# Attention and feed-forward block: keys and queries turned together, their operands filled by transfers, bias and shift rows turned on VectorE

## The reference, cut to what matters

```python
q = rmsnorm((x @ Wq) per head, q_rms_w);  k = rmsnorm((x @ Wk) per head, k_rms_w);  v = (x @ Wv) per head
gate = softplus(einsum('bthd,hd->bht', k, u_n) / 8)
bias = -dist * softplus(omega) * slope * gate        # dist = max(i - j, 0), gate at key j
attn = softmax(q k^T / 8 + bias, causal)
x = layernorm(x + (attn v) @ Wproj)
x = layernorm(x + ffn(x))
```

## Time and profile before

| | |
|---|---|
| time, median of 3 runs | 3689.66 us (3685.36 to 3691.62) |
| the profiled execution, its own time | 3688.23 us |
| its span, first to last instruction | 3686.4 us |
| TensorE busy | 3318.4 us (90%) |
| VectorE, ScalarE, GpSimd busy | 1923.1 (52%), 1868.7 (51%), 1518.6 us (41%) |
| mean granted TensorE clock | 0.954 of 2.4 GHz |
| attention, 92 to 2500 us | TensorE busy 2156 of 2408 us |

### The profile page before, as it was taken

How to read it: one execution, slowest core, us unless ns; L and a number is a source line. 1 busy time by engine, 2 the same in 40 slices (tenths; PEclk the granted TensorE clock), 3 DMA queues, 4 the chain that set the end, 5 groups by cost and what they waited for, 6 DMA issues and landing times. The chain is left out here.

```text
span 3686.4 us, 46240 instructions
## 1 busy us (share of the span) xinstructions
PE 3318.4 (90%) x16112; PEld 2537.8 (69%) x16112; DVE 1923.1 (52%) x4064; ACT 1868.7 (51%) x3185; POOL 1518.6 (41%) x1318
## 2 busy tenths in 40 slices
PE   4989989889899898898988989877999999899999
PEld 3756757667576675665766757656888787688887
DVE  6576566665766757656666576623222222233232
ACT  1666666666666666665666666653222222232222
POOL 4556556555565565555655556541111111000000
PEclk7999999999999999999999999988999999899999
DMA  1111111111112011011111110124222222221120
GB/s 53 32 40 24 37 31 30 38 25 31 40 37 48 24 37 39 22 36 31 30 38 25 31 40 23 37 72 134 83 83 83 83 89 86 70 97 59 45 69 18
DMA packets 138680, 179.90 MB, mean 49 GB/s; under 512 B 37712, under 2 KB 70096, under 8 KB 138448
## 3 DMA queue, kind: packets, MB, share of 16 engines
q1 hardware_dynamic: 138448, 176.94, 17.3%
HBM read 83.81 MB, written 42.47 MB: 34 GB/s over the span
## 5 line engine op out<-in xcount | busy, mean ns | idle before, releaser
L340 POOL TENSOR_TENSOR e_lo<-e_all,e_hi 128x512 fp32r<-128x512 f32 (+1 forms) x832 | 1041.7, 1257 | 948.4 <-ACT e_all L566 792.3
L566 ACT ACTIVATE e_all<-ps_s,bias 128x512 f32<-128x512 f32 (+3 forms) x1280 | 781.4, 619 | 183.5 <-PE ps_s L865 120.5
L559 ACT ACTIVATE e_hi<-ps_s,bias 128x512 fp32r<-128x512 f32 (+1 forms) x832 | 557.7, 670 | 326.9 <-PE ps_s L863 212.8
L747 DVE TENSOR_REDUCE maxes<-ps_m 128x1 f32<-128x512 f32 x768 | 525.2, 686 | 364.0 <-PE ps_m L838 359.6
L838 PE MATMUL ps_m<-k_ext,q_max 128*128 128x512 f32 (+3 forms) x1280 | 486.2, 393 | 61.5 <-DVE maxes L747 38.7
L862 PE MATMUL ps_s<-q_twice,k_split 128*128 128x512 f32 (+3 forms) x1280 | 493.3, 385 | 0.0
L863 PE MATMUL ps_s<-q_ext,k_ext 128*128 128x512 f32 (+3 forms) x1280 | 480.4, 375 | 0.0
L896 PE MATMUL ps_v<-e_lo,v_main 128*66 128x512 f32 (+1 forms) x832 | 441.2, 530 | 15.6 <-POOL e_lo L340 15.6
L838 PEld LDWEIGHTS ps_m<-k_ext,q_max 128*128 128x128 f32 x1280 | 249.5, 195 | 213.3 <-DVE maxes L747 75.2
L744 DVE CUSTOM_DVE_ANT_0 ps_m<-ps_m,mask_row 128x128 f32<-128x128 f32 (+3 forms) x512 | 252.4, 493 | 247.5 <-PE ps_m L838 243.5
L885 PE MATMUL ps_v<-e_hi,v_main 128*66 128x512 f32 (+1 forms) x832 | 331.5, 398 | 0.0
(11 more groups left out here) (211 smaller groups left out, 6517.4 us busy)
## 6 DMA issues: line engine op xcount, KB each, us to landing
q_twice<-q_max SPq DMA_DIRECT2D x256, 128.0 KB, 2.3
yt<-y_out SPq DMA_DIRECT2D x128, 130.0 KB
k_split<-k_ext SPq DMA_DIRECT2D x128, 128.0 KB, 2.2
y_in<-yt SPq DMA_DIRECT2D x128, 128.0 KB, 3.1
r_in<-recip_sums SPq DMA_DIRECT2D x128, 128.0 KB, 3.2
hidden<-gelu SPq DMA_DIRECT2D x64, 256.0 KB, 2.0
a_in<-hidden SPq DMA_DIRECT2D x8, 2048.0 KB, 10.5
x_tok<-in_L_attn_x_dram SPq DMA_DIRECT2D x8, 512.0 KB, 4.8
```

Source lines behind the costliest of these rows:

```text
L340: on.tensor_tensor(e_lo[:, i % LO_RING, off:QB], e_all[:, u_ % E_RING, off:QB], e_hi[:, i % HI_RING, off:QB].bitcast(F32), ALU.subtract).t ...
L559: nc.scalar.activation(e_hi[:, i % HI_RING, off:QB], ps_s[u_ % 2][:, off:QB], ACT.Exp, bias=by).then_inc(hi_done, 1)
L566: nc.scalar.activation(e_all[:, u_ % E_RING, off:QB], ps_s[u_ % 2][:, off:QB], ACT.Exp, bias=by).then_inc(ex_done, 1)
L747: nc.vector.tensor_reduce(maxes[:, qt, kc:kc + 1], ps_m[m % 2][:, 0:width], AX.X, ALU.max).then_inc(mx_free, 1)
```

## The change

- Keys and queries of a head lie beside each other in `raw` (128 columns), and one turn of four transposes brings both; a head has 4 turns, due 0.066 apart, in place of 8 due 0.033 apart.
- ScalarE writes the hi parts of both into `kq_hi`, VectorE the lo parts into `kq_lo` (two buffers each). Transfers on SyncE's queue bring them to `k_ext`, `q_max`, `k_split` (hi) and `k_split`, `q_ext` (lo): five in place of one. The first `max` of a block now waits for `hi_dup`, the landing of the three hi transfers, where it waited for ScalarE.
- The 4 bias columns of each key part leave `raw` (2 columns of logits remain, so 386 in place of 392). VectorE transposes them in blocks of 32 x 32 once a pair, four transfers store them in DRAM (`rows_dram`), and one for each head brings them into `k_ext`. The first `max` of a head also waits for that one.
- The shift row is transposed on VectorE in blocks of 32 x 32; four transfers bring it in place of one. TensorE has no `shift` step any more.
- `project`, `turn` and the transposes of the second batch (`x`) alternate between the banks `ps_p` and `ps_t`, and each waits for the step two before.

```diff
-NTURN = 2 * NQB
+NTURN = NQB
+SQ = 32
...
-            turns = [first + 0.005 + 0.033 * i for i in range(NTURN)]
+            turns = [first + 0.005 + 0.066 * i for i in range(NTURN)]
             for i, when in enumerate(turns):
                 at(when, "turn", n, i)
-            start, end = (turns[1] + 0.03, t0 + 0.28) if s == 0 else (t0 + 0.29, t0 + 1.29)
+            start, end = (turns[0] + 0.07, t0 + 0.28) if s == 0 else (t0 + 0.29, t0 + 1.29)
             for v, (qt, kc) in enumerate(MAXES):
                 qb = qt // TQ
-                when = max(start + (end - start) * v / (NM - 1), turns[2 * qb + 1] + 0.03)
+                when = max(start + (end - start) * v / (NM - 1), turns[qb] + 0.07)
                 at(when, "max", n, v)
                 if v + 1 == maxes_to(qb):
                     at(when + 0.001, "most", n, qb)
-                    at(when + 0.03, "shift", n, qb)
+                    at(when + 0.002, "shift", n, qb)
...
+        works = [s for s in steps if s[0] in ("project", "turn") or s[0] == "x" and s[1] == 1]
+        work_no = {step: i for i, step in enumerate(works)}
+        GATE = 2 + 8 + 14 + 2 + 2 + 1
...
-        def project_bank(p, t):
-
-            return ps_v[1] if p == 0 and t % 2 else ps_p
+        def work_bank(step):
+            return (ps_p, ps_t)[work_no[step] % 2]
+
+        def work_free(eng, step):
+
+            if work_no[step] < 2:
+                return
+            kind, a, b = works[work_no[step] - 2]
+            if kind == "x":
+                eng.wait_ge(xt_done, NXT * a + b + 1)
+            if kind == "project":
+                eng.wait_ge(pj_free, TT * a + b + 1)
+            if kind == "turn":
+                eng.wait_ge(tr_free, NTURN * a + b + 1)
 
...
                     sp.dma_start(w_in[:, :, CV:WCOLS], wv[:, cols].rearrange("(k p) c -> p k c", p=P)).then_inc(w_load, 16)
                     for s in range(2):
                         head = p % (H // 2) * 2 + s
-                        sp.dma_start(w_in[:, :, k_cols(s):k_cols(s) + D],
-                                     wk[:, head * D:(head + 1) * D].rearrange("(k p) c -> p k c", p=P)).then_inc(w_load, 16)
+                        for c, w in ((k_cols(s), wk), (q_cols(s), wq)):
+                            sp.dma_start(w_in[:, :, c:c + D], w[:, head * D:(head + 1) * D].rearrange("(k p) c -> p k c", p=P)).then_inc(w_load, 16)
+                if step[0] == "gate b" and step[2] == GATE_PARTS - 1:
+                    p = step[1]
+                    sp.wait_ge(gate, GATE * (p + 1))
+                    for i in range(2):
+                        if p >= 1:
+                            sp.wait_ge(rows_in[i], 16 * p)
+                    for a in range(P // SQ):
+                        sp.dma_start(rows_dram.rearrange("c r a j -> a r c j")[a],
+                                     bias_out[a * SQ:(a + 1) * SQ, :].rearrange("r (c j) -> r c j", j=SQ)).then_inc(rows_out, 16)
                 if step[0] == "turn":
-                    n, i = step[1:]
-                    s, qc = n % 2, i // 2
-                    if i % 2 == 0:
-                        cols = slice(qc * QB, (qc + 1) * QB)
-                        sp.wait_ge(qk_hi, NTURN * n + i + 1)
-                        sp.dma_start(k_split[s][0:D, cols].bitcast(F32), k_ext[s][0:D, cols].bitcast(F32)).then_inc(k_dup[s][qc], 16)
+                    n, qb = step[1:]
+                    s, i = n % 2, NTURN * n + qb
+                    cols = slice(qb * QB, (qb + 1) * QB)
+                    sp.wait_ge(qk_hi, i + 1)
+                    sp.dma_start(k_ext[s][0:D, cols].bitcast(F32), kq_hi[i % 2][0:D, :].bitcast(F32)).then_inc(hi_dup[i % 2], 16)
+                    sp.dma_start(q_max[s][0:D, cols].bitcast(F32), kq_hi[i % 2][D:P, :].bitcast(F32)).then_inc(hi_dup[i % 2], 16)
+                    if qb == 0:
+                        sp.wait_ge(rows_out, 16 * (P // SQ) * (n // 2 + 1))
+                        sp.dma_start(k_ext[s][R_BIAS:R_BIAS + NBIAS, :].bitcast(F32), rows_dram[:, s * TT:(s + 1) * TT, :, :].rearrange("c r a j -> c (r a j)")).then_inc(rows_in[s], 16)
+                    sp.dma_start(k_split[s][0:D, cols].bitcast(F32), kq_hi[i % 2][0:D, :].bitcast(F32)).then_inc(hi_dup[i % 2], 16)
+                    sp.wait_ge(tr_free, i + 1)
+                    sp.dma_start(k_split[s][D:P, cols].bitcast(F32), kq_lo[i % 2][0:D, :].bitcast(F32)).then_inc(lo_dup[i % 2], 16)
+                    sp.dma_start(q_ext[s][0:D, cols].bitcast(F32), kq_lo[i % 2][D:P, :].bitcast(F32)).then_inc(lo_dup[i % 2], 16)
                 if step[0] == "twice":
                     n, qb = step[1:]
                     s, grp = n % 2, n * NQB + qb
                     cols = slice(qb * QB, (qb + 1) * QB)
-                    sp.wait_ge(qk_hi, NTURN * n + 2 * qb + 2)
+                    turned(sp, n, qb)
...
+                    sp.wait_ge(shifted, grp + 1)
+                    for a in range(P // SQ):
+                        row = q_ext[n % 2][R_SHIFT:R_SHIFT + 1, qb * QB:(qb + 1) * QB].bitcast(F32).rearrange("o (t p) -> o t p", t=TQ)
+                        sp.dma_start(row[:, :, a * SQ:(a + 1) * SQ], shift_rows[grp % 2][a * SQ:a * SQ + TQ, :]).then_inc(row_in[grp % 2], 16)
...
+                    n, qb = step[1:]
+                    i = NTURN * n + qb
+                    act.wait_ge(tr_full, i + 1)
+                    if i >= 2:
+                        act.wait_ge(hi_dup[i % 2], 48 * (i // 2))
+                        act.wait_ge(tr_free, i - 1)
+                    nc.scalar.activation(kq_hi[i % 2][:], work_bank(step)[:], ACT.Copy, scale=qk_w[:, 0:1]).then_inc(qk_hi, 1)
                 if step[0] == "scores":
                     n, v = step[1:]
                     u_ = NU * n + v
@@ -607,7 +647,7 @@
...
+                        glink(nc.vector.tensor_copy(bias_in[:, :, 0, :, :], c_jc[:]))
+                        glink(nc.vector.tensor_tensor(bias_in[:, :, 1, :, :], c_jc[:], bias_in[:, :, 0, :, :].bitcast(F32), ALU.subtract))
+                        if p >= 1:
+                            dve.wait_ge(rows_out, 16 * (P // SQ) * p)
+                        glink(nc.vector.transpose(bias_out[:], bias_in[:].rearrange("p x h s t -> p (x h s t)").bitcast(F32)))
                         assert gated[0] == GATE * (p + 1), gated[0]
                 if step[0] == "bias":
...
+                    n, qb = step[1:]
+                    i = NTURN * n + qb
+                    dve.wait_ge(qk_hi, i + 1)
+                    if i >= 2:
+                        dve.wait_ge(lo_dup[i % 2], 32 * (i // 2))
+                    nc.vector.scalar_tensor_tensor(kq_lo[i % 2][:], work_bank(step)[:], qk_w[:, 0:1], kq_hi[i % 2][:].bitcast(F32),
+                                                   ALU.mult, ALU.subtract).then_inc(tr_free, 1)
...
                     n, qb = step[1:]
                     dve.wait_ge(mx_free, NM * n + maxes_to(qb))
-                    if n >= 1:
-                        dve.wait_ge(tr_full, turn_no["shift", n - 1, qb] + 1)
-                    nc.vector.tensor_reduce(neg_max[:, qb * TQ:(qb + 1) * TQ], maxes[:, qb * TQ:(qb + 1) * TQ, 0:qb + 1],
+                    grp = n * NQB + qb
+                    if grp >= 2:
+                        dve.wait_ge(shifted, grp - 1)
+                    nc.vector.tensor_reduce(neg_max[grp % 2][:, 0:TQ], maxes[:, qb * TQ:(qb + 1) * TQ, 0:qb + 1],
                                             AX.X, ALU.max, negate=True).then_inc(nm_done, 1)
...
-                    dve.wait_ge(tr_full, turn_no[step] + 1)
+                    dve.wait_ge(nm_done, grp + 1)
                     if grp >= 2:
-                        dve.wait_ge(row_in[grp % 2], 16 * (grp // 2))
-                    nc.vector.tensor_copy(shift_rows[:, grp % 2, :], ps_t[0:TQ, 0:P]).then_inc(tr_free, 1)
+                        dve.wait_ge(row_in[grp % 2], 16 * (P // SQ) * (grp // 2))
+                    nc.vector.transpose(shift_rows[grp % 2][:], neg_max[grp % 2][:].bitcast(F32)).then_inc(shifted, 1)
...
                 if step[0] == "turn":
-                    n, i = step[1:]
-                    s = n % 2
...
+                    n, qb = step[1:]
+                    col = k_cols(n % 2)
...
-                    if turn_no[step]:
-                        pe.wait_ge(tr_free, turn_no[step])
-                    col, width = ((k_cols(s), KCOLS), (s * D, KCOLS))[i % 2]
+                    work_free(pe, step)
                     for t in range(TQ):
-                        last = nc.tensor.transpose(ps_t[0:width, t * P:(t + 1) * P], raw[:, (i // 2) * TQ + t, col:col + width], ident[:])
+                        last = nc.tensor.transpose(work_bank(step)[:, t * P:(t + 1) * P], raw[:, qb * TQ + t, col:col + 2 * D], ident[:])
                     last.then_inc(tr_full, 1)
...
-                        pe.wait_ge(qk_hi, NTURN * n + 2 * (qt // TQ) + 2)
+                        turned(pe, n, qt // TQ)
+                        if qt == 0:
```

(53 more changed lines are left out.)

96 lines of the change are left out of this document (37 added, 59 removed).

## The result

The changed kernel takes 3590.43 us (median of 4 runs, 3587.56 to 3598.06) where the kernel before, beside it, takes 3689.14: the ratio is 0.9737, with a 95% interval of 0.9719 to 0.9754. The forecast was 3595, the range 3560 to 3665. The profiled execution has a span of 3588.1 us.

What follows compares the result with a forecast made beforehand. TensorE's work and waits were taken to bound attention, except ahead of the gate, where VectorE paces. 77.5 + 61.0 - 6 - 32 (landings) - 3 (gate chain) - 3 (first pair) = 94.5 us saved: 3595 us, range 3560 to 3665.

Steps and rivals of the forecast that it cites:

- Two stages: Attention pair: savings count in the 120 us TensorE paces, not in the 30 us ahead of the gate, where VectorE is full.
- one of the signs: Ahead of the gate: the prediction is wrong if the 30 us of VectorE's stage change length.
- Work, 77.5 us: TensorE in attention: fewer turns save 58.9 us, shift transposes gone 14.6 us, narrower projection 4 us.
- Waits, 61.0 us less 6: TensorE's waits for ps_t and negative maxima that count go, 61.0 us; 6 us return as waits for ScalarE or VectorE.
- rival 4: Saved work reappears as waits for VectorE, whose stage ahead of the gate begins earlier: 3673 us, chance 0.07.
- Landings, 2.0 us a pair: Even head's first max of blocks 0 and 1 waits for transfers: cost 32 us, ends 18 and 86.
- the walk: SyncE's queue from the gate, issue by issue: stalls of 0 to 0.4 and 1.1 to 1.5 us at blocks 0 and 1.
- Gate chain, +0.2 us a pair: VectorE's last instructions before the gate: casts and subtractions become one each plus a block transpose, costing 3 us.
- DMA pieces of 128 bytes: Bias stores and shift rows: short pieces expected to land no later than 2 KB ones, against the skill's 512-byte rule.
- rival 5: Short pieces make store and load of the bias rows slow, 3.4 us more before the first max: 3649, chance 0.03.
- The sum: Whole kernel: the terms together save 94.5 us, giving a forecast of 3595 us.
- Of the rivals, 2: Landings, with stalls near 5.4 us a pair, take the gain back in large part: 3662 us, chance 0.20.

Runs made afterwards that it cites:

- e4: Changed kernel with six max matmuls of each odd head, just ahead of the gate, made four times instead of once: 3599.9 us, ratio 0.9773.
- e5: Changed kernel with six max matmuls of each odd head, in the middle of the even head's scores, made four times: 3650.2 us, ratio 0.9906.
- e10: Changed kernel with the shift row transposed on TensorE again, copied by VectorE and moved by one transfer: 3604.4 us, ratio 0.9772.
- e3: Changed kernel with every turn's four transposes made twice into the same place: 3632.9 us, ratio 0.9847.
- e1: Kernel before the change, with only project, turn, shift and the second batch's transposes alternating between two banks: 3629.1 us, ratio 0.9832.
- e6: Changed kernel with the first max of a block due 0.12 of a head behind its turn, not 0.07: 3563.0 us, ratio 0.9668.
- e7: Changed kernel with the first max of a block due 0.03 of a head behind its turn, not 0.07: 3642.1 us, ratio 0.9883.
- e11: Changed kernel with the even head's turns due 0.38 of a head before its start, not 0.46: 3578.3 us, ratio 0.9705.

## Why the prediction was right, and where its terms were not

**Two stages.** Right, and shown by e4 and e5: the same kind of matmuls cost next to nothing in a pair ahead of the gate and 3.4 us elsewhere. e10 shows the same of waits. The stage kept its length, which was one of the signs: from the end of the first wait for maxima to the gate it is 26.0 us before the change and 25.3 after it (mean of 15 pairs).

**Work, 77.5 us.** e3 gives a turn 0.42 us of busy time (53.5 us in all; 42 us of device time) where I had 0.46 (58.9); e10 gives the shifts 13 us with their waits where I had 14.6 + 3.7. The 4 us of the narrower projection were not tested. TensorE's busy time fell by 102 us, more than 77.5. A part may be time around a wait that counts as busy: in e1 it fell by 15 us with no instruction less. The rest stays open.

**Waits, 61.0 us less 6.** The waits went and were worth 58 us alone (e1). But the 6 us that I took back was the term mis-sized most: waits for maxima rose by 39.5 us, by 47 outside the 30 us ahead of a gate, and the wait at the gate by 38 where 28 was forecast, so all of TensorE's waits in attention together did not fall. 33 us of them show behind the odd head's turns, 24 to 55 us behind the gate, where these two stand in the pair shown and others like them in the rest:

```profile
1399.35 0.50 PE L879 MATMUL ps_m<-k_ext,q_max 128*128 128x512 f32 x1 [1.30 <-DVE maxes L786]
...
1404.26 0.50 PE L879 MATMUL ps_m<-k_ext,q_max 128*128 128x512 f32 x1 [0.84 <-DVE maxes L786]
```

With the pause for `ps_t` gone, TensorE reaches VectorE's next maximum sooner; no run here takes VectorE's work away there, so this reading is argued from the trace and not shown. It is what rival 4 said in part, that saved work comes back as waits for VectorE, though it had them ahead of the gate.

**Landings, 2.0 us a pair.** Right in place, less than I took in size: 0.27 and 1.54 us in the pair shown, which is above the mean, and 22.3 us in all, 4.2 us of it in the first pair. The other 15 pairs have 1.2 us each, near the low end of the walk's 1.1 to 1.9. The first `max` of block 1 waits in all of them, that of block 0 in only 5. e6 and e7 show that the landings are on the path; the later due time gives 27 us back, 1.7 a pair, and the clock is a part of that. Odd heads and block 2 show none, and outside the first pair none is over 2.2 us.

**Gate chain, +0.2 us a pair.** Near for an undisturbed chain, wrong in sign on the mean. From the end of the last norm to the last gate instruction's end it is 1.29 us in all 16 pairs after the change. Before it, it is 1.19 us in 10 pairs and 2.8 to 2.9 us in 6, in the mean 1.8, so the change gains 0.5 us a pair, some 8 us. The block transposes take 0.31 us (128 x 128) and 0.21 us (128 x 32). In each of the 6 pairs two instructions of the end took 0.9 to 1.25 us beside GpSimd. After the change, then one of the 6 before it, then one of the 10:

```profile
1355.43 2.67 POOL L366 TENSOR_TENSOR e_lo<-e_all,e_hi 128x512 fp32r<-128x512 f32 x2 [0.87 <-ACT e_all L606]
...
1360.76 0.19 DVE L749 TENSOR_TENSOR c_jc<-g,omega_eff 128x32 f32<-128x32 f32 x1
1360.98 0.19 DVE L751 TENSOR_TENSOR c_jc<-c_jc,key_no 128x32 f32<-128x32 f32 x1
...
1361.70 0.31 DVE L757 STREAM_TRANSPOSE bias_out<-bias_in 128x128 f32<-128x128 f32 x1
```

```profile
1262.71 2.66 POOL L340 TENSOR_TENSOR e_lo<-e_all,e_hi 128x512 fp32r<-128x512 f32 x2 [0.40 <-ACT e_all L566]
...
1263.33 1.17 DVE L708 TENSOR_TENSOR raw<-g,omega_eff 128x32 f32<-128x32 f32 x1
1264.53 0.92 DVE L710 TENSOR_TENSOR raw<-raw,key_no 128x32 f32<-128x32 f32 x1
```

```profile
964.07 0.22 DVE L708 TENSOR_TENSOR raw<-g,omega_eff 128x32 f32<-128x32 f32 x1
964.32 0.22 DVE L710 TENSOR_TENSOR raw<-raw,key_no 128x32 f32<-128x32 f32 x1
```

TensorE now stands 5.9 us at the gate, and GpSimd has run out of work at 1358.1 and holds nothing up. The two go together in every pair: before the change TensorE waits 1.7 to 2.7 us at the gate in the 6 pairs with the long end and 4.2 us or more in the others, and in e10 the end is 2.96 us in the 5 pairs with a wait of 1.9 to 2.2 us, 1.96 us in the 2 pairs with 3.1, and 1.3 us in those with 3.3 or more. A TensorE that comes early and waits long leaves the end of the chain undisturbed. This is the reverse of what e11 ran into.

**DMA pieces of 128 bytes.** The bias stores land after 1.5 us, sooner than any transfer shown before, and no `max` waits for the load of the rows, so rival 5 is out. The rule of the Trainium skill (DMA: Bandwidth & Descriptors, Specifications) on pieces below 512 bytes doesn't show in transfers of 16 KB.

**The sum.** It came within 5 us, by errors that cancel, and that closeness is luck: work and the gate chain gave more than I took, the landings cost less, waits for maxima took much more. In place of 77.5 + 61.0 - 6 - 32 - 3 - 3 the trace gives, roughly, 102 + 61 - 47 - 22 + 8 = 102 us where 98.7 were measured; it is rough, since a part of the 102 us lies ahead of gates. Of the rivals, 2 was alive: at a due time of 0.03 (e7) the gain is half.

## What to carry to other kernels

Before pricing a removed instruction or wait, cut the period into stages by which engine is full, and price it only where its engine is the full one; padding one engine with the same work in each stage shows the cut at once. When an operand goes through a transfer in place of a copy, the queue decides: count every issue between the data and the last needed transfer, and give the consumer's due time that much room, since here 0.05 of a head later gained 27 us and 0.04 sooner cost 52. A filler that keeps one engine from waiting can lengthen the chain it waits for, through a third engine (read from the traces, e11 above all). And look for waits again after some are removed: here TensorE's idle time in attention was 249 us where it had been 252, at other places.

## What was not expected of the hardware

- VectorE's small instructions with tensors in SBUF took 0.19 to 0.22 us alone and up to about 1.2 us while GpSimd's 1.3 us `e_lo` ran, in the kernel before, the changed one and e11.
- Short waits can cost clock beyond their length: 18 us of waits removed (e6) came with 31 us less at 1.2 GHz between 150 and 2300 us, 14 of them in the 30 us behind a gate, where the removed waits stood.
- A transfer of a row of the shift costs SyncE 0.57 us to issue for 0.5 KB, as much as one of 128 KB (0.46 to 0.60 us).
